# Normalization, turning and q/k/v projection of each chunk in one block, with the next chunk's turning ahead of the last one's products

## The reference, cut to what matters

```python
def _ln_c(v, eps=1e-06):
    m = jnp.mean(v, axis=-1, keepdims=True)
    s = jnp.var(v, axis=-1, keepdims=True)
    return (v - m) / jnp.sqrt(s + eps)
...
    qkv = x @ qkv_w.T + qkv_b
...
    rel_h = jnp.einsum('bnhwc,hkc->bnhwk', r_q, Rh)
    rel_w = jnp.einsum('bnhwc,wkc->bnhwk', r_q, Rw)
...
    x = x + _L0_conv_ref(_ln_c(x), ...)
    t = t + _L0_ffn_ref(_ln_t(t), ...)
    x = x + _L1_conv_ref(_ln_c(x), ...)
    t = t + _L1_ffn_ref(_ln_t(t), ...)
```

## Time and profile before

| | us |
|---|---|
| three runs | 3319.51, 3325.30, 3328.25 (median 3325.30) |
| profiled execution: its own time | 3325.34 |
| profiled execution: span | 3323.8 |

### The profile page before, as it was taken

The page is one execution under the profiler, slowest core; times in us unless marked ns, Lnnn a source line. Parts: engine busy times, 40 slices in busy tenths (PEclk is TensorE's granted clock), DMA queues, the critical chain, the costliest instruction groups (busy, mean ns, idle before and its releaser), DMA issues. The chain is left out here.

```text
span 3323.8 us, 62798 instructions
## 1 busy us (share of the span) xinstructions
PE 2587.4 (78%) x18516; PEld 1200.4 (36%) x18516; DVE 2460.0 (74%) x4648; ACT 1861.5 (56%) x2594; POOL 502.0 (15%) x559
## 2 busy tenths in 40 slices
PE   4749999997499227389999956188888859499998
PEld 2512222226499215122222233011111147266666
DVE  6878999975755348689999855599999645465665
ACT  3526777782255116167777736077777825555554
POOL 1210211111333523101111100101111100000000
PEclk9859999996699659599999977599999979699999
DMA  2575677754122213766666601112122110200000
GB/s 59 188 144 112 143 143 149 151 116 145 34 78 77 69 30 136 172 118 151 142 141 149 145 17 55 55 41 62 57 62 62 48 32 1 71 6 5 9 5 14
DMA packets 208983, 281.99 MB, mean 85 GB/s; under 512 B 56606, under 2 KB 100366, under 8 KB 208842
## 3 DMA queue, kind: packets, MB, share of 16 engines
q1 hardware_dynamic: 169258, 216.05, 28.0%
q0 software_dynamic: 19920, 31.57, 4.0%
q10 hardware_dynamic: 19664, 32.60, 3.3%
HBM read 201.65 MB, written 77.46 MB: 84 GB/s over the span
## 5 line engine op out<-in xcount | busy, mean ns | idle before, releaser
L804 DVE TENSOR_REDUCE c0att_mx<-c0att_m 128x1 f32<-128x512 f32 x768 | 493.4, 685 | 34.0 <-PE c0att_m L741 28.7
L804 DVE TENSOR_REDUCE c1att_mx<-c1att_m 128x1 f32<-128x512 f32 x768 | 493.5, 685 | 32.1 <-PE c1att_m L741 27.0
L804 DVE TENSOR_REDUCE f1att_mx<-f1att_m 128x1 f32<-128x512 f32 x768 | 480.1, 682 | 21.1 <-PE f1att_m L741 18.9
L1053 ACT ACTIVATE c0att_p<-c0att_s 128x1024 f32<-128x1024 f32 x384 | 373.9, 1020 | 150.1 <-PE c0att_s L757 150.0
L1053 ACT ACTIVATE c1att_p<-c1att_s 128x1024 f32<-128x1024 f32 x384 | 373.9, 1020 | 148.6 <-PE c1att_s L757 148.5
L1053 ACT ACTIVATE f1att_p<-f1att_s 128x1024 f32<-128x1024 f32 x384 | 373.2, 1020 | 121.3 <-PE f1att_s L757 121.3
L741 PE MATMUL f1att_m<-f1att_km,f1att_qm 48*128 48x512 f16 x768 | 156.3, 402 | 155.6 <-DVE f1att_mx L804 99.6
L1483 ACT ACTIVATE moe_h<-moe_u,moe_bu 128x512 f32<-128x512 f32 x192 | 136.5, 711 | 175.9 <-PE moe_u L1400 93.8
L770 PE MATMUL c0att_o<-c0att_p,c0att_vs 128*32 128x512 f32 x1536 | 206.3, 609 | 0.6 <-ACT c0att_p L1053 0.6
L741 PE MATMUL c1att_m<-c1att_km,c1att_qm 64*128 64x512 f16 x768 | 156.1, 402 | 64.5 <-DVE c1att_mx L804 34.9
L770 PE MATMUL f1att_o<-f1att_p,f1att_vs 128*32 128x512 f32 x1536 | 205.6, 607 | 0.7 <-ACT f1att_p L1053 0.5
(11 more groups left out here) (623 smaller groups left out, 5323.9 us busy)
## 6 DMA issues: line engine op xcount, KB each, us to landing
xt<-rel_parts SPq DMA_DIRECT2D x256, 128.0 KB, 5.1
xt<-qk_parts SPq DMA_DIRECT2D x192, 128.0 KB, 4.4
y<-rel_parts SPq DMA_DIRECT2D x128, 128.0 KB, 5.2
y<-qk_parts SPq DMA_DIRECT2D x96, 128.0 KB, 4.7
c0att_qm<-rel_parts SPq DMA_DIRECT2D x144, 64.0 KB, 2.1
c1att_qm<-rel_parts SPq DMA_DIRECT2D x144, 64.0 KB, 2.1
f1att_ka<-qk_parts SPq DMA_DIRECT2D x144, 64.0 KB, 2.1
expert_rows<-y SPq DMA_DIRECT2D x39, 192.0 KB, 2.0
```

What stands on the lines that cost most here:

```text
L804: dve.tensor_reduce(mx[:, n:n + 1], bank[:, :], AX.X, ALU.max).then_inc(s_mx, 1)
L1053: act.activation(pr[h][kt % 2][:, :], sps[h][:, :], ACT.Exp).then_inc(s_e, 1)
```

## The change

- `start`, `layer_norm` (for `c0ln`, `c1ln` and `h`) and `qkv` are replaced by one function `front`, once for each attention. In it the chunk is the unit of everything: while PE does the products of chunk c-1, chunk c is turned and the moments of chunk c+1 are made. The queues are in order: PE has the turning of chunk c, then the units of c-1; DVE has `low_parts(c)`, `prepare(c+1)`, `finish(c+1)`, `take(c-1)`; ACT has `high_parts(c)`, `by_column(c-2)`, `normalize(c+1)` and three `high_of(c-1, g)`.
- Moments are made for 8 tiles at a time (c0, f1) or 4 (c1), instead of 32. In c1 and f1 ACT normalizes (L616), in c0 DVE (L518).
- The bias of q and k is a sixth product of the unit, on a row of ones, and the scale of q is put on the weights. ACT's fp32 copy `qt` is gone: DVE makes `low` from the bank itself (L537).
- The rearrangement by columns is ACT's alone, 6 operations a chunk (L645); POOL has none.
- The banks of q/k and of v are 3 and 3 (4 and 4 before), since one pair holds turned tiles; the position phase has 8 (4 before).
- In c1 the gather, the adding and `bn_stats` of `routed_experts` are in `front`, with a ring of 4 chunks for the gathered rows.
- In c0 the loads of x are four, one per image, ahead of the weights on SP's queue, and other constants come by POOL's queue. In f1 POOL's queue stores the keys, 24 of the 48 transfers.
- The block no longer waits for the stores to land; `attention` waits for them where it reads. The order of its pairs is changed: first the pairs of heads 0 to 5 of all four images, then those of heads 6 to 11; SP's and POOL's loops are split accordingly.

```diff
-def qkv(nc, name, parts, vt, w, scratch, spare=None):
...
-        qp = [m.ps(f"qp{u}") for u in range(2)] + rp[0:2]
-        vp = [m.ps(f"vp{u}") for u in range(2)] + rp[2:4]
...
-                for c in range(CHUNKS):
-                    pool.wait_ge(s_v, 4 * c + 4)
-                    for g in range(GROUPS):
-                        pool.wait_ge(s_hi, c * GROUPS + g + 1)
-                        pool.tensor_copy(by_columns(by_x[g][0:GW, :], c), by_rows(high, c, g)).then_inc(s_byx[0], 1)
...
-                for c in range(CHUNKS):
-                    for g in range(GROUPS):
-                        turned(c, g)
-                        values(4 * c + g)
-                    values(4 * c + GROUPS)
...
-                        dve.tensor_tensor(low[:, cols], qt[n % 3][:, :], high[:, cols], ALU.subtract).then_inc(s_lo, 1)
...
-                        act.activation(qt[n % 3][:, :], qp[n % 4][:, :], ACT.Identity, bias=bias[:, g:g + 1],
-                                       scale=gain[:, 0:1]).then_inc(s_qt, 1)
-                        act.activation(high[:, at(c, g)], qp[n % 4][:, :], ACT.Identity, bias=bias[:, g:g + 1],
-                                       scale=gain[:, 0:1]).then_inc(s_hi, 1)
...
-                sp.wait_ge(s_st, 64 * B * GROUPS)
-                if rel:
-                    for k in range(2):
-                        for u in range(2):
-                            sp.wait_ge(s_rst[k][u], 256 * (2 - u))
+def front(nc, name, src, eps, stats, parts, ident, vt, w, scratch, kept, spare=None, load=None, back=None, hidden=None):
...
+    SET = TC if back else 2 * TC
+    by_act = load is None
+    LAG = 4
...
+        qp = [m.ps(f"qp{u}") for u in range(3)]
+        vp = [m.ps(f"vp{u}") for u in range(3)]
+        rp = qp + vp + [t0, t1]
...
+                if not rel:
+                    for b in range(B):
+                        for g in range(GROUPS):
+                            pool.wait_ge(s_lo, (2 * b + 1) * GROUPS + g + 1)
+                            store_qk(pool, b, g, 1, kept["keys"])
...
+                def gather(c):
+                    if c >= LAG:
+                        pool.wait_ge(s_add, 2 * TC * (c - LAG + 1))
+                    for k in range(2):
+                        for j in range(TC):
+                            t = c * TC + j
+                            pool.indirect_dma_start(
+                                ring[c % LAG][k][:, j * C:(j + 1) * C], None, scratch["yd"][:, :],
+                                bass.IndirectOffsetOnAxis(back["give"][:, k * TILES + t:k * TILES + t + 1], 0)
...
+                def turn_over(c):
+                    pe.wait_ge(s_norm, TC * (c + 1))
+                    if c:
+                        pe.wait_ge(s_xlo, 2 * c)
...
+                    if c < CHUNKS:
+                        turn_over(c)
+                    if c:
+                        for g in range(GROUPS):
+                            turned(c - 1, g)
+                            values(TC * (c - 1) + g)
+                        values(TC * (c - 1) + GROUPS)
...
+                def spread(first, count, center, done):
+                    s = slice(first, first + count)
+                    dve.tensor_tensor(center[:, s], half[:, 1, s], half[:, 4, s], ALU.add).then_inc(s_mom, 1)
+                    dve.tensor_tensor(mdiff[:, s], half[:, 1, s], half[:, 4, s], ALU.subtract).then_inc(s_mom, 1)
+                    dve.scalar_tensor_tensor(out=vsum[:, s], in0=half[:, 2, s], scalar=C * eps, in1=half[:, 5, s],
+                                             op0=ALU.add, op1=ALU.add).then_inc(s_mom, 1)
...
+                def prepare(c):
+                    if back:
+                        dve.wait_ge(back["sems"][c], 16 * 2 * TC)
+                        for k in range(2):
+                            if k:
+                                dve.wait_ge(s_add, 2 * TC * c + TC)
+                            for j in range(TC):
+                                t = TC * c + j
+                                cols = slice(t * C, (t + 1) * C)
+                                dve.scalar_tensor_tensor(out=src[:, cols], in0=ring[c % LAG][k][:, j * C:(j + 1) * C],
+                                                         scalar=back["top"][:, k * TILES + t:k * TILES + t + 1],
+                                                         in1=src[:, cols], op0=ALU.mult, op1=ALU.add).then_inc(s_add, 1)
+                        dve.wait_ge(s_add, 2 * TC * (c + 1))
+                    if TC * c % SET:
+                        return
+                    tiles = range(TC * c, TC * c + SET)
+                    if load:
+                        dve.wait_ge(s_x[c // 2], 16)
+                    if hidden:
+                        for t in tiles:
+                            dve.tensor_scalar(src[:, ts(t, C)], hidden["x"][:, ts(t, C)], mean0[:, t:t + 1],
+                                              rstd0[:, t:t + 1], ALU.subtract, ALU.mult).then_inc(s_inner, 1)
+                        dve.wait_ge(s_inner, TC * c + SET)
+                    for t in tiles:
+                        dve.bn_stats(stats[:, ts(t, 6)], src[:, ts(t, C)]).then_inc(s_stats, 1)
+                    dve.wait_ge(s_stats, TC * c + SET)
+                    spread(TC * c, SET, mean, TC * c // SET + sets)
...
+                def finish(c):
+                    if TC * c % SET == 0:
+                        settle(TC * c, SET, mean, rstd, TC * c // SET + sets)
+                    if by_act:
+                        return
+                    dve.wait_ge(s_rstd, 5 * (TC * c // SET + sets + 1))
+                    if c >= 2:
+                        dve.wait_ge(s_turned, c - 1)
+                    for j in range(TC):
+                        t = TC * c + j
...
+                def low_parts(c):
+                    cols = slice(c * CHUNK, (c + 1) * CHUNK)
+                    dve.wait_ge(s_xhi, 2 * c + 2)
+                    if hidden:
+                        dve.wait_ge(s_f32, 2 * c + 2)
+                    upper, under = (t[:, cols] for t in hidden["turned"]) if hidden else (t0[:, :], t1[:, :])
+                    dve.tensor_tensor(xa_lo[:, cols], upper, xa_hi[:, cols], ALU.subtract).then_inc(s_xlo, 1)
+                    dve.tensor_tensor(xb[C1:P, cols], under[0:C1, :], xb[0:C1, cols], ALU.subtract).then_inc(s_xlo, 1)
...
+                def take(c):
+                    for j in range(TC):
+                        t = TC * c + j
+                        b, kt = t // KT, t % KT
+                        if j < GROUPS:
+                            n, cols = c * GROUPS + j, at(c, j)
+                            dve.wait_ge(s_hi, n + 1)
+                            dve.scalar_tensor_tensor(out=low[:, cols], in0=qp[n % 3][:, :], scalar=1.0 / W_SCALE,
+                                                     in1=high[:, cols], op0=ALU.mult, op1=ALU.subtract).then_inc(s_lo, 1)
+                        dve.wait_ge(s_v, t + 1)
...
+                for c in range(CHUNKS + 1):
+                    if c < CHUNKS:
+                        low_parts(c)
+                    if c + 1 < CHUNKS:
+                        prepare(c + 1)
+                        finish(c + 1)
+                    if c:
+                        take(c - 1)
...
+                def normalize(c):
+                    if TC * c % SET == 0:
+                        root(TC * c, SET, TC * c // SET + sets)
+                    if not by_act:
+                        return
+                    act.wait_ge(s_rstd, 5 * (TC * c // SET + sets + 1))
+                    if c >= 2:
+                        act.wait_ge(s_turned, c - 1)
+                    for j in range(TC):
+                        t = TC * c + j
+                        act.activation(nrm[c % 2][:, j * C:(j + 1) * C], src[:, ts(t, C)], ACT.Identity,
+                                       bias=away[:, t:t + 1], scale=rstd[:, t:t + 1]).then_inc(s_norm, 1)
...
+                    act.activation(high[:, at(c, g)], qp[n % 3][:, :], ACT.Identity,
+                                   scale=1.0 / W_SCALE).then_inc(s_hi, 1)
...
+                def by_column(c):
+                    act.wait_ge(s_v, TC * (c + 1))
+                    act.wait_ge(s_lo, GROUPS * (c + 1))
+                    act.wait_ge(s_hi, GROUPS * (c + 1))
+                    for g in range(GROUPS):
+                        for rows, buf in ((slice(0, GW), high), (slice(GW, P), low)):
+                            act.activation(by_columns(by_x[g][rows, :], c), by_rows(buf, c, g),
+                                           ACT.Identity).then_inc(s_byx, 1)
...
+                for c in range(CHUNKS + 1):
+                    if c < CHUNKS:
+                        high_parts(c)
+                    if rel and c > 1:
+                        by_column(c - 2)
+                    if c + 1 < CHUNKS:
+                        normalize(c + 1)
+                    if c:
+                        for g in range(GROUPS):
```

(27 more changed lines are left out.)

477 lines of the change are left out of this document (243 added, 234 removed).

## The result

The changed kernel takes 3272.6 us in the median of 4 runs (3270.7 to 3274.9), the kernel before 3324.3 beside it: a ratio of 0.9845, with a 95% interval of 0.9828 to 0.9862. It is 52 us faster, where 92 were forecast (3233). The time lies in the stated range of 3206 to 3280, but only in its widened part: the forecast's own range ended at 3266. The profiled execution has a span of 3271.1 and a time of 3273.2, and the sum can be settled against it.

A forecast was written before the change was run, and what follows sets the result against it. DVE was taken to bound `c1ln` and `c1qkv`, stores the position phase. Gains of 16.6 and 1 (c0), 46 and 1 (c1) and 28 (f1), together 92.6, took 3325.30 to 3233 us; range 3206 to 3266, widened to 3280.

The forecast's parts named there:

- the slow end: Slow case: c0 8, c1 2, f1 5 us more, 3248; with 0.7 us more hand-over in 22 periods, 3264.
- B: Rival: in c1 gathers starve beside a busy DVE, a chunk takes 20.6 us for 15.4; about 3285, chance 0.06.
- C: Rival: slower, with "remote" gaps of 4.2 us in 22 periods costing 92; two per period give 3417; chance 0.04.
- D: Rival: stages only join, each chunk waiting for its predecessor's `take`, 2.6 us more waits per period; 3290, chance 0.09.
- the price of `by_column`: ACT's six rearranging operations of 64x512 per chunk, taken at 0.5 to 0.6 us each, 3.0 to 3.6 together.
- the cover of 6.6 us: In c1, DVE's adding and moments, 6.6 us per chunk, beside which `by_column` was to lie hidden.
- the 3.8: In c0, the tables' DVE work, now inside the loop, added to the sum as an estimate of 3.8 us.
- the half clock: PE in c1 taken at half clock because idle over half the period: period 15.4 us, 14.1 at full clock.
- The tail: End of c1: last `low_parts`, two `take`s with PE's last units between them, and the tables, 11 us.
- f1's end: Two queues store while f1's chunks run, leaving some 7 us of stores behind: 2077 against 2104.9, -28 us.
- The 61 us: Store-bound stretch from last `low` to SP's last `rel_parts` issue in c0 and c1, 61 us each, expected to stay.
- The order of pairs: Attention's reordered pairs, costed at nothing: loads and work per pair the same, first maxima waiting behind DVE's constants.

The follow-up runs named there:

- experiment 1: Changed kernel with ACT's six rearranging operations per chunk reading neighbouring elements instead of jumping by 16, so the rearrangement itself is left out: 3241.4 us.
- 2: Changed kernel with only the order of ACT's work in c0's loop altered, same work and results: 3256.8 us.
- 8: Changed kernel with the position phase of c0 and c1 using 4 banks in place of 8: 3272.6 us.
- 9: On top of experiment 7, ACT's rearranging of the last chunk moved behind the first eight evictions of the position phase: 3225.6 us.
- experiment 7: Changed kernel with ACT's work reordered in c0, c1 and f1, and in c0 POOL rearranging the high q rows: 3223.7 us.

## Why the prediction was right, and why by half only

- **The forecast.** The sign and the mechanism held in c1 and f1: c1 gains 47.5 us from the first gather to the last low, f1 22.5 behind its last low, and c0's first stretch loses 8.4 of it. That the time fell into the range at all is in part luck: c0 alone missed by 27 us where the slow end had 8 for it. DVE was to be over 85% busy in c1; it is busy 49.7 of 76.2 us (1161.93 to 1238.10), 65%, and the prices gave 11.1 of 15.4 themselves.
- **The rivals.** B did not come: 64 gathers have a mean of 0.975 us beside a busier DVE, as before, 1.26 from start to start, 10.1 a chunk under a period of 15.2. The trap of the Trainium skill's page "SBUF — State Buffer", section "SBUF: two separate sides", is for a DVE operation in a mode that takes both ports; beside this block's additions, statistics and evictions the trace shows no such delay. C did not come either: no wait marked "remote" stands in the `front` of c1, whose DVE waits all end on ACT once the first rows have landed. D is out in c1 and f1 by the periods. In c0 DVE did wait as D wanted: its periods are 2.8 and up to 4.9 us over mine, where D needs 2.6, and the total is nearer to D's 3290 than to 3233. But the cause is another: experiment 1 takes most of these waits away and 2 a part, and both leave the ring of hand-overs as it is.
- **The term that was mis-sized** is the price of `by_column`: "0.5 to 0.6 each, 3.0 to 3.6", measured 1.15 and 6.9. It was priced by the shape of its rows, not by how it reads, and on the path of a chunk it stands for c1 only, with a cover; in c0's sum it has no term. In c1 the cover of 6.6 us nearly held it (period 15.2, forecast 15.4, 14.8 at the old price). In c0 there is no adding, so it stood ahead of root and evictions on ACT's queue. Of the 27 us there, experiment 1 gives 21 back at the old price, and 2 gives back 14 with the price as it is and the order changed. The 6 that are left under 1 lie behind the last `low_parts`: 13.9 us to the last `low`, where I had 8.3, one period and the last `take`. Its first `low_parts` and its periods are 4.1 us over mine together, and the 3.8 that I had added for the tables' work make up for them.
- **The prices that held.** Normalizing on ACT was taken at 0.44 and is 0.44 in a row (1.86 for 4, with 0.54 for one alone); two `low_parts` 1.44; `take` 2.9; first `low_parts` of c1 22.8 us behind the gather's start (forecast 22.6); PE at half clock in the turning; a period in f1 17.1 with moments (forecast 16.2) and 6.7 to 8.5 without (7.6). The reason given for the half clock, PE idle over half of the period, is not in the rows: from 1177.16 to 1192.39 PE is busy 9.4 of 15.2 us, at a mean granted clock of 0.75.
- **The tail.** I ended c1 11 us behind the last `low_parts`, the trace has 19.8: two turns in which the six operations stand ahead of `high_of` with nothing beside them. These are 8.8 us too many; seven periods of 103.7 for my 107.8 take 4.1 back, so that c1's stretch is over by 4.9. c0 ends in the same way, with 19.8 us for my 8.3.
- **f1's end** was the second step that failed: "some 7 us of stores stay behind it", measured 14.1. The landing of the last stores, which I counted as gone, is waited for by all engines at attention's first instruction.
- **The 61 us** behind the last `low` were misread in the rows of before: they are 58.7 and 58.3, and 57.3 and 57.8 after. So these stages stayed, as forecast. With the rows read rightly the sum would have been 4.7 us lower, and further from the time measured. The 8 banks count for nothing (8); whether an earlier start would count is not shown (9).
- **The order of pairs** was costed at nothing. From c1's attention to f1's first moments it is 605.0 in the profile of the changed kernel, 601.0 before, and 601.1 to 604.7 in the profiles of experiments that leave it alone. An effect of 0 to 4 us can't be told from their scatter; going back to the old order was not tried.

The differences between the last two columns of the table are 27.3, -3.5, -1.4, 4.9, -2.7, 4.0, 2.3, 7.1 and 2.4, together 40.4: the whole gap between the forecast's span and the one measured.

## What to carry to other kernels

When work moves from one engine to another, look for its own rows on the engines that it leaves as well as for rows of the same shape on the engine that it comes to, and where they differ (here 0.6 to 1.5 us) carry the whole range into the sum: neither is a price for the new engine. In a ring of in-order queues ask of each piece of filler what stands behind it in its queue, and check the cover chunk type by chunk type: at its true price in place of the old one the same six operations cost 0.5 us a period in c1, 6 us in the tail of either block, and 21 us in all of c0. A wait that a block no longer has at its end is gone only if the next block does not begin with it.

## What the runs showed of the hardware that I had not expected

- ACT's time for a 64x512 fp16 copy within SBUF depends on how it reads: 627 ns for neighbouring elements, 1126 ns where each is 16 elements (32 bytes) from the last. DVE's copy with the same jump took 0.61 us alone, and POOL's 1465 ns on average before, beside a full DVE, and 1145 ns in experiment 7.
- A `low` of DVE that read two tiles of SBUF took 0.87 to 1.33 us wholly beside one of POOL's copies, and 0.68 alone (before). The `low` that reads a PSUM bank and one tile of SBUF took at most 0.69 beside them (experiment 7).
- Behind the last `low` of f1, stores of q and k from two queues keep the DMA engines busy 0.52 to 0.74 of the time at 120 to 145 GB/s, from SP's alone 0.26 at 96 to 102 GB/s: the share of busy time is no measure of what is moved.
